# Wide products with a zero operand between the steps of a recurrent loop on TensorE

## What is computed

```python
def step(carry, xs):
    h, c = carry
    xi_t, xf_t, xg_t, xo_t = xs
    i_t = jax.nn.sigmoid(xi_t + h @ V_i)
    g_t = jnp.tanh(xg_t + h @ V_c)
    o_t = jax.nn.sigmoid(xo_t + h @ V_o)
    c_new = h * c + i_t * g_t
    h_new = o_t * jnp.tanh(c_new)
    return ((h_new, c_new), h_new)
(_, _), hs = lax.scan(step, (h0, c0), (xi, xf, xg, xo))
```

## Time and profile before

| what | value |
|---|---|
| median of three executions | 22905.64 us |
| span of the profiled execution | 21044.8 us |
| of it the recurrent loop, from 10290 to 20943 us | about half of the span |
| steps in the loop | 6250 |
| TensorE products busy in the span | 13995.6 us (67%) |
| VectorE busy | 11084.8 us (53%) |
| ScalarE busy | 7314.8 us (35%) |

### The profile page before, as it was taken

How to read it: one execution, slowest core, us unless ns; L and a number is a source line. 1 busy time by engine, 2 the same in 40 slices (tenths; PEclk the granted TensorE clock), 3 DMA queues, 4 the chain that set the end, 5 groups by cost and what they waited for, 6 DMA issues and landing times. The chain is left out here.

```text
span 21044.8 us, 693677 instructions
## 1 busy us (share of the span) xinstructions
PE 13995.6 (67%) x249248; PEld 10710.3 (51%) x249249; DVE 11084.8 (53%) x57746; ACT 7314.8 (35%) x56155; POOL 6038.7 (29%) x6537
## 2 busy tenths in 40 slices
PE   5426778832885666566677777777777777777776
PEld 3211236521453444444466666666666666666665
DVE  6325666651114555555555555555555555555555
ACT  0006851100111010010355555555555555555554
POOL 0676666675713767757200000000000000000000
PEclk9558987755997777777555555555555555555555
DMA  0000012211002333333200000000000000000000
GB/s 29 17 5 5 1 31 82 81 20 50 23 25 69 105 94 102 104 90 105 39 4 4 4 4 4 4 4 4 4 4 4 4 4 4 4 4 4 4 4 15
DMA packets 346132, 611.36 MB, mean 29 GB/s; under 512 B 153661, under 2 KB 224158, under 8 KB 342332
## 3 DMA queue, kind: packets, MB, share of 16 engines
q0 software_dynamic: 251520, 473.04, 9.0%
q1 hardware_dynamic: 91708, 99.21, 1.4%
HBM read 507.49 MB, written 64.29 MB: 27 GB/s over the span
## 5 line engine op out<-in xcount | busy, mean ns | idle before, releaser
L2049 PE MATMUL lr_Z<-ls_h,ls_V 128*128 128x1 f16 x225000 | 7176.0, 166 | 2912.4 <-DVE ls_h L2097 2832.3
L2049 PEld LDWEIGHTS lr_Z<-ls_h,ls_V 128*128 128x128 f16 x225000 | 6664.8, 105 | 3912.0 <-DVE ls_h L2097 3830.0
L2091 DVE SCALAR_TENSOR_TENSOR ls_c<-ls_S,ls_hc 128x1 f32<-128x1 f32 x12500 | 2370.5, 220 | 3550.9 <-ACT ls_S L2067 3550.9
L2066 ACT ACTIVATE ls_S<-lr_Z 128x1 f32<-128x1 f32 x12500 | 2070.3, 171 | 5186.3 <-PE lr_Z L2049 5186.3
L2010 POOL COPY ls_HT<-ls_h 128x250 f32 x50 | 19.8, 395 | 10697.1 <-DVE ls_h L2099 10697.1
L630 PE MATMUL prop_sum<-prop_G,prop_S 128*128 128x256 f32 x5040 | 1890.4, 554 | 1342.8 <-DMA prop_G<-hop_table,prop_idx 1202.4
L616 POOL DMA_INDIRECT prop_G<-hop_table,prop_idx x2520 | 2388.5, 948 | 1194.3 <-issue 727.3
L630 PEld LDWEIGHTS prop_sum<-prop_G,prop_S 128*128 128x128 f32 x5040 | 1424.7, 290 | 1808.5 <-issue 942.5
L2097 DVE TENSOR_TENSOR ls_h<-ls_S,ls_th 128x1 f16<-128x1 f32 x12500 | 1888.8, 163 | 808.2 <-ACT ls_th L2074 10.8
L2074 ACT ACTIVATE ls_th<-ls_c 128x1 f32<-128x1 f32 x12500 | 2094.2, 199 | 0.0
L2071 ACT ACTIVATE ls_S<-lr_Z 128x1 f32<-128x1 f32 x12500 | 2068.4, 171 | 0.6 <-issue 0.5
(11 more groups left out here) (407 smaller groups left out, 14494.3 us busy)
## 6 DMA issues: line engine op xcount, KB each, us to landing
prop_G<-hop_table,prop_idx POOLq DMA_INDIRECT x2520
hop_table<-ht_T SPq DMA_DIRECT2D x75, 256.0 KB, 2.1
me_W<-in_L_ffn_W SPq DMA_DIRECT2D x16, 1024.0 KB, 10.8
moe_out<-me_Ys SPq DMA_DIRECT2D x108, 128.0 KB, 1.7
gm_AG<-gat_atable,gm_idx POOLq DMA_INDIRECT x840
gs_G<-gat_table,gs_idx POOLq DMA_INDIRECT x840
sd_records<-sc_ring_recsd,sc_ring_placesd POOLq DMA_INDIRECT x784, 2.1
ss_records<-me_ring_recss,me_ring_placess POOLq DMA_INDIRECT x432, 2.1
```

What stands on the lines that cost most here:

```text
L2049: mm = nc.tensor.matmul(Z[hf][bank][:, col:col + 1], (V2 if part == "21" else V1)[:, q, ROWS.index(row), :], hx[:, prev, q:q + 1], start=F ...
L2066: nc.scalar.activation(S[:, s % 2, m:m + 1], Z[hf][m][:, col:col + 1], ACT.Sigmoid, scale=back)
L2091: nc.vector.scalar_tensor_tensor(c[:, e, m:m + 1], S[:, e, KD + m:KD + m + 1], S[:, e, m:m + 1], hc[:, m:m + 1], ALU.mult, ALU.add).then_i ...
```

## The change

TensorE gets further wide products in each step. A tile `none` of 128 x 125 float16 zeros is made in the first phase by GpSimd. After the narrow products of a step and the one of `ahead`, if the step has one, a function `idle` issues products of `V1`'s first block with `none`, so many that each step has five wide products in all: four beside one of `ahead`, five in the other steps. They write the odd columns of bank 3 of the other set, which nothing reads, in the same stride of two as `ahead`. Two products of 250 zero columns before the loop start these banks.

```diff
+IDLE = 5
...
+        none = ph.sb("none", [P, HALF], F16)
...
+                    nc.gpsimd.memset(none[:], 0.0)
...
+                    def idle(hf, count):
+
+                        for _ in range(count):
+                            o = Z[hf][BANKS - 1][:, 0:KD * HALF].rearrange("p (t m) -> p t m", m=KD)[:, :, 1]
+                            nc.tensor.matmul(o, V1[:, 0, 0, :], none[:], start=False, stop=False, skip_group_check=True)
+
+                    for hf in range(2):
+                        nc.tensor.matmul(Z[hf][BANKS - 1][:, 0:KD * HALF], V1[:, 0, 0, :], none[:, 0:1].broadcast_to([P, KD * HALF]),
+                                         start=True, stop=False, skip_group_check=True)
                     for a in range(len(AHEAD)):
                         ahead(a, 0, 0)
...
                             for a in range(s % HALF * PER, min(len(AHEAD), (s % HALF + 1) * PER)):
                                 ahead(a, i * BODY + HALF * (hf + 1), 1 - hf)
+                            idle(1 - hf, IDLE - len(range(s % HALF * PER, min(len(AHEAD), (s % HALF + 1) * PER))))
```

## The result

The changed kernel took 24863.81 us (median of four, 24840.05 to 24952.37) against 22905.93 us for the kernel before on the same chip: a ratio of 1.0871, 95% interval 1.0846 to 1.0896, 1958 us more. The prediction was 24890 us.

A forecast was written before the change was run, and what follows sets the result against it. The prediction took each step's chain as the bound, with TensorE waiting for h1, and TensorE as the new bound after the change. 22906 us plus 1988 (1875 for the period, 120 for the bias's steps, less 7) gave 24890, range 24500 to 25250.

The forecast's parts named there:

- The bound and its chain: In the loop, 10.65 ms at clock 0.50: each step a closed chain of 1.70 us, TensorE idle 0.55 awaiting h1.
- The price of a wide product, 0.208 us: Each zero product in the loop costs 0.208 us, like the strided 125-column products back to back ahead of the loop.
- The period, 2.21 + 0.94 - 1.15 = 2.00 us: Loop step from narrow products' start S: last wide ends S+2.21, next narrow end 0.94 later, quiet ones S+1.15; 0.30 us more.
- The 0.94 us: Time from the last wide product's end to the last narrow one's end behind a queue, read behind the 48 products.
- The bias's steps, 0.20 us more: In the 600 steps whose wide product is the bias's, an estimated 0.20 us each on top, 120 us.
- The sum, 1988 us: Loop loss: 6250 x 0.30 = 1875 us plus 120, less 7 hidden where the loop goes round.
- The clock: Granted clock stays 0.50 in the loop; the rival has it rise to 1.00, 22530 us, 9 in 100.
- The bridge between span and timed runs: The median's 1861 us above the profile's span taken as outside the loop and untouched, so 1988 was added to the median.
- Hidden zero products: Rival: zero products in the loop cost the contiguous price, 0.10 us, period stays 1.70, 22906 us; 5 in 100.
- each waits for the one before: Rival: each zero product in a step waits for its predecessor, 0.32 us apart, up to 27590 us; 3 in 100.

The follow-up runs named there:

- r10: The kernel before, with h2 made per half straight from sigmoid, tanh and h1, no zero products: 20915.25 us against 21057.17, ratio 0.9935.
- r3: The changed kernel with four wide products per step in place of five: 21767.68 us, ratio 1.0332 to the kernel before.
- r2: The changed kernel with zero products writing 125 neighbouring columns in place of every second one: 21124.6 us against 21069.5 for the kernel before, ratio 1.0026.
- r4: The changed kernel with the added products multiplying input data in place of zeros: 23059.25 us, ratio 1.0944 to the kernel before.
- r6: The kernel before with neighbouring-column sums, six 262-column zero products per step (five beside the bias's), 40 before the loop, 24 per round: 24925.96 us, ratio 1.1843.
- r8: The kernel before with neighbouring-column sums, six zero products per step, 128-row bias products, 28 more zero products each third step of 250: 22874.65 us, ratio 1.0001.
- r11: r8 with h2 made per half as in r10: four executions took 22498 to 23634 us, against 21057 us for the kernel before.

## Why the prediction was right

- **The bound and its chain.** Right. The loop was worth 10.7 ms at clock 0.50, and the wait of TensorE for `h1` was the room that the zero products had. The chain held one thing more, which the prediction did not see: the narrow products wait for `h2` as well, and r10 has 142 us from that.
- **The price of a wide product, 0.208 us.** Right, 0.207 from r3 to the changed kernel, and for the reason given: r2 takes the stride away and the price halves, r4 shows that zeros play no part. One reading in it was off without harm: of six back to back the last takes 0.50 us to pass and not 0.39, but it is their ends that stand 0.208 us apart, from the first one's on, and that gives the same sum.
- **The period, 2.21 + 0.94 - 1.15 = 2.00 us.** Right to a hundredth, 1.79 and 1.70 with four and three products as well. The 0.94 us, read once at the loop's entry, held in all 6150 steps away from the rounds. The places within the step are 0.07 us off: behind a queue the wide product starts at S+1.08 and the narrow ones end at S+1.22, where the prediction took 1.01 and 1.15 from a step without one. The period takes the one less the other, so this cancels.
- **The bias's steps, 0.20 us more.** Right, 2.20 us: the bias's product starts 0.07 us later than another (S+1.15 against S+1.08), and the last zero product ends at S+2.48 against S+2.28.
- **The sum, 1988 us.** The loop itself took 1988 us more by the traces. That this agrees to the last figure is luck, since a hundredth in the period is 62 us. The rounds of the loop are not free, as the prediction had them, but cost 0.14 us more each, 3 us in all. The executions give 1958 us on the chip of the result, with an interval of some 57 us to either side, and 1990 on r4's.
- **The clock.** It stayed at 0.50, as it had in the 48 products ahead of the loop; what lifts it the prediction did not know, and r6 and r8 each show a stretch that did. One condition of the rival was wrong: that with a clock of 1.00 in the first steps all of the loop would run so. r6 has 1.00 there and falls back in its third step. The price of the full clock was mis-sized too: I took 0.06 us per step from TensorE's rows alone, and r8 has 0.024 by the raw starts, where the wait for `h2` had grown from 27 to 63 ns. Of the Trainium skill's rule (TensorE: Matmul & The Clock Gate, What's actually happening), that activity lifts the clock, the traces show that a TensorE busy 99.6% of the loop (the first window above) can be at 0.50 all the same.
- **The bridge between span and timed runs.** Wrong: the 1861 us lay in the part ahead of the loop, on another chip, not outside the span. The span forecast with it, 23035 us, was 24875.3. The 24890 us were not harmed, since the difference was added to the timed median.
- **The other rivals.** Hidden zero products needed the contiguous price: r2 shows that case, at 1.0026. That each waits for the one before did not occur.

## What to carry to other kernels

An idle engine's wait is room for work only up to its length, so price the filler by its own form at the clock that is granted now, not at the one hoped for: three products here were free, the fourth and fifth cost 0.09 and 0.21 us in each of 6250 steps. Write a product's output into neighbouring columns wherever the reader does not mind. And before buying a faster clock, ask what is late next: r8 had it for the whole loop and won nothing, while removing a wait of 27 ns for VectorE gave 0.65%.

## What the runs showed of the hardware that I had not expected

- The same steps run at either clock: in r11, steps 18 to 80 of a round ran at 1.00, in 1.65 us each, in 14 of the 25 rounds, where the clock was still up from the stretch of 28, and at 0.50, in 2.24 us each, in the other 11. In r8 they kept 1.00 in every round.
- A halt of TensorE of only 0.16 to 0.18 us stood ahead of each loss of the clock in r11, while in the changed kernel a TensorE busy 99.6% of the loop stayed at 0.50.
- At the full clock narrow products hardly come faster: 36 take 1.04 us in r6 against 1.14 at 0.50 later in the same loop, while wide ones of 262 columns halve, from 0.219 to 0.112 us apart by their raw starts.
- A product with 128 rows behind one with a single row starts 0.32 us after it (15005.16 and 15005.48 in the profile after), where one behind a product of 128 rows starts 0.08 us after that (15003.09 and 15003.17).
- The chips of these runs differ by 1.84 ms in the part of this kernel ahead of the loop and hardly in the loop (12681.2 and 12682.3 us): the kernel before took 21049 to 21069 us on some, 22884 to 22906 us on others. A ratio of two runs on different chips would have been worthless here.
